# Expert rows written to DRAM in slot order ahead of the experts, loaded back in quarters of the partitions and transposed by VectorE

## The reference

```python
def _moe_forward(x, gate_w, w_gate_up, w_down, shared_w_gate_up, shared_w_down):
    x2 = x.reshape(-1, orig_shape[-1])
    g_s, u_s = jnp.split(x2 @ shared_w_gate_up.T, 2, axis=-1)
    shared_out = jax.nn.silu(g_s) * u_s @ shared_w_down.T
    probs = jax.nn.softmax(x2 @ gate_w.T, axis=-1)
    topk_vals, topk_idx = jax.lax.top_k(probs, 2)
    topk_vals = topk_vals / jnp.sum(topk_vals, axis=-1, keepdims=True)
    combine = jnp.sum(jax.nn.one_hot(topk_idx, 16) * topk_vals[..., None], axis=1)
    g, u = jnp.split(jnp.einsum('th,eih->eti', x2, w_gate_up), 2, axis=-1)
    out_e = jnp.einsum('eti,ehi->eth', jax.nn.silu(g) * u, w_down)
    return (jnp.einsum('eth,te->th', out_e, combine) + shared_out).reshape(orig_shape)

x = x + tanh(g_xattn[0]) * xattn(layernorm(x), ctx, ...)
x = x + tanh(g_ffn[0]) * ffn(layernorm(x), ...)
```

## Time and profile before

| | |
|---|---|
| time, median of 3 runs | 1397.36 us (1397.26 to 1397.74) |
| profiled execution | 1397.51 us, of which 1395.8 us are its span |
| busy share of the span | PE 99%, DVE 72%, ACT 37%, POOL 26% |
| expert blocks | from 1198 to 1345 us of the span |
| granted TensorE clock, mean | 0.999 |

### The profile page before, as it was taken

How to read it: one execution, slowest core, us unless ns; L and a number is a source line. 1 busy time by engine, 2 the same in 40 slices (tenths; PEclk the granted TensorE clock), 3 DMA queues, 4 the chain that set the end, 5 groups by cost and what they waited for, 6 DMA issues and landing times.

```text
span 1395.8 us, 26753 instructions
## 1 busy us (share of the span) xinstructions
PE 1382.0 (99%) x8757; PEld 1121.7 (80%) x8758; DVE 1000.4 (72%) x2135; ACT 514.6 (37%) x1117; POOL 358.0 (26%) x374
## 2 busy tenths in 40 slices
PE   9999999999999999999999999999999999999998
PEld 7888887888888887888887888888787888777777
DVE  6444456888888888888888888888688746244458
ACT  5333444333333434343333333343434331222242
POOL 1121223221212121212211121212122100367646
PEclk9999999999999999999999999999999999999999
DMA  6544431111111111111101111111123244555548
GB/s 220 189 128 143 128 109 44 39 42 31 49 31 43 39 42 32 43 40 41 43 30 47 36 42 32 49 31 42 54 72 98 99 151 174 188 196 165 165 154 298
DMA packets 91238, 125.52 MB, mean 90 GB/s; under 512 B 7184, under 2 KB 57360, under 8 KB 90896
## 3 DMA queue, kind: packets, MB, share of 16 engines
q1 hardware_dynamic: 83632, 99.70, 22.7%
q0 software_dynamic: 7520, 24.65, 5.3%
HBM read 86.84 MB, written 37.49 MB: 89 GB/s over the span
## 4 chain that ended last, share of the span: by engine, by line
PE 79%; DVE 3%; issue 1%; DMA 1%; ACT 0%; DVEq 0%; POOL 0%; SPq 0%; ACTq 0%
PE ps L609 19%; PE ps L611 18%; PE ps L610 18%; PE ps L1004 6%; PE ps L696 5%; PE ps L743 4%; PE ps L1020 3%; PE ps L728 2%; PE ps L999 1%; DVE acc L1960 1%; DVE acc L1967 1%; DMA y<-ybuf 1%; PE ps L917 1%; PE ps L751 0%; PE ps L1051 0%
## 5 line engine op out<-in xcount | busy, mean ns | idle before, releaser
L506 POOL CAST vth<-vt 128x256 fp32r<-128x256 f32 x64 | 25.4, 397 | 541.4 <-PE ps L743 539.4
L1194 ACT CAST ah<-ps 128x256 fp32r<-128x256 f32 x256 | 83.4, 383 | 187.5 <-PE ps L611 181.0
L609 PE MATMUL ps<-hT,w0h 128*128 128x512 f32 (+1 forms) x384 | 152.2, 396 | 0.0
L611 PE MATMUL ps<-hT,w0h 128*128 128x512 f32 (+1 forms) x384 | 149.9, 390 | 0.0
L610 PE MATMUL ps<-hT,w0l 128*128 128x512 f32 (+1 forms) x384 | 149.6, 390 | 0.0
L500 POOL TENSOR_TENSOR qr<-qv,mhalf 128x8 f32<-128x8 f32 x64 | 105.1, 1642 | 151.5 <-DVE qv L1560 124.3
L1511 DVE TENSOR_TENSOR acc<-ps,acc 128x512 f32 (+1 forms) x128 | 88.0, 687 | 56.6 <-PE ps L611 56.4
L1160 ACT COPY qs<-ps 128x512 f32<-128x512 f32 x128 | 75.3, 588 | 122.6 <-PE ps L611 122.6
L1172 ACT ACTIVATE pb<-pb 128x256 f32<-128x256 f32 x128 | 48.3, 418 | 167.0 <-DVE pb L1578 166.9
L609 PE MATMUL ps<-w0l,ah 128*128 128x512 f32 x256 | 105.6, 413 | 0.0
L609 PE MATMUL ps<-w1l,ah 128*128 128x512 f32 x256 | 104.9, 410 | 0.0
(11 more groups left out here) (250 smaller groups left out, 3216.1 us busy)
## 6 DMA issues: line engine op xcount, KB each, us to landing
wraw<-in_w_att SPq DMA_DIRECT2D x64, 256.0 KB, 2.7
vbuf<-vo SPq DMA_DIRECT2D x16, 512.0 KB, 3.3
kbuf<-ko SPq DMA_DIRECT2D x16, 512.0 KB, 3.8
kt<-kbuf SPq DMA_DIRECT2D x32, 256.0 KB, 2.9
vt<-vbuf SPq DMA_DIRECT2D x64, 128.0 KB, 2.2
wgu<-in_w_gu SPq DMA_DIRECT2D x4, 2048.0 KB, 9.0
y<-ybuf SPq DMA_DIRECT2D x16, 512.0 KB, 7.1
xt<-in_x SPq DMA_DIRECT2D x16, 256.0 KB, 4.2
```

Source lines behind the costliest of these rows:

```text
L609: pe.matmul(dst, l_hi, r_lo, start=first, stop=False)
L611: return pe.matmul(dst, l_hi, r_hi, start=False, stop=last)
L1194: act.copy(ah[:, bp, :, b2, :], pv_view(bp, b2)).then_inc(a_hi, 1)
```

## The change

Instead of gathering each block's rows by an index just ahead of their use, the kernel writes all rows to DRAM in slot order once. After the slot numbers are known, GpSimd scatters each token tile twice (for the first and the second expert) from four row buffers `rows` in SBUF to `xbuf`, 32 indirect DMAs by `sli`. SP loads those tiles from `h2buf` into `rows`: the first four when the logits have been transposed, the others as scatters of the buffer's last tile have landed (`rows_out`). `rows` lies in memory that place 0 of `act_raw` uses later, so VectorE waits for all scatters ahead of `shared_in(3, 0)`. Slots which no token fills must hold finite numbers, so SP copies rows of `x` over the whole of `xbuf` during attention, 28 copies of 512 KB.

A block is then loaded by SP with plain DMAs, one for each quarter q of 32 partitions. To make that enough, `h2` tiles are stored with their columns in another order (`by_quarter`): the four values of the four parts of the width stand side by side. A quarter of a row in DRAM is then what 32 partitions of the transposed block need, and VectorE turns each block with one 32x32-block transpose (`turn_rows`), straight into `xgT`. TensorE's four transposes and ScalarE's copy go, and ScalarE copies the down product to `ye` in VectorE's place.

Around it: the logits' transposes stand half a step earlier on TensorE, and `shared_in(1, 1)` stands behind the first part of the routing on VectorE. The last shared step runs its first part for both halves first, after which `xgT` may be written. Some semaphores are joined to keep their number; these waits ask for the same events as before.

```diff
+    xbuf = nc.dram_tensor("xbuf", [(STEPS - NC) * P, D], F32, kind="Internal").ap()
+    x_rows = xbuf.rearrange("(b g i) (q n) -> b q i g n", g=4, i=32, q=4)
+    x_pair = xbuf.rearrange("(d r p) n -> d r p n", r=2, p=P)
...
+        with ExitStack() as a:
+            sb("below_rows", [P, 2 * 4096], F32, a)
+            rows = [sb(f"rows{q}", [P, D], F32, a) for q in range(4)]
...
+        def by_quarter(t):
+            return t.rearrange("p (m k) -> p k m", k=KD)
+        def in_order(t):
+            return t.rearrange("p (k m) -> p k m", k=KD)
...
             with sp.Fori(0, (STEPS - NC) // 2) as d:
                 for odd in range(2):
                     next_loads(d, odd)
+                sp.dma_start(x_pair[d], x[0:2]).then_inc(x_in, 16)
...
+            def load_rows(n):
+                if n >= 4:
+                    sp.wait_ge(rows_out[n % 4], 32 * (n // 4))
+                sp.dma_start(rows[n % 4][:], h2_t[n]).then_inc(rows_in[n % 4], 16)
+
+            def load_block(b, j):
+                if not isinstance(b, int) or b >= 3:
+                    sp.wait_ge(xgT_done, b - 2)
+                for q in range(4):
+                    src = x_rows[b, q] if isinstance(b, int) else x_rows[bass.ds(b, 1), q].rearrange(
+                        "a i g n -> (a i) g n")
+                    sp.dma_start(xg[j % 3][32 * q:32 * q + 32, :].rearrange("p (g n) -> p g n", g=4), src).then_inc(
+                        xg_in[j % 3], 16)
...
-            pool.wait_ge(sidx_ok, 1)
-            for q in range(4):
-                pool.wait_ge(h2_stored[q], 16 * (NT // 4) + 16)
-            def gather(b):
...
+            pool.wait_ge(slot_ok, 1)
+            for n in range(NT):
+                pool.wait_ge(rows_in[n % 4], 32 + 16 * (n // 4))
+                for z in range(2):
+                    pool.indirect_dma_start(xbuf, bass.IndirectOffsetOnAxis(sli[:, z, n:n + 1], 0),
+                                            rows[n % 4][:], None).then_inc(rows_out[n % 4], 16)
...
-                    mm = pe.transpose(PS[bank][:, k * P:(k + 1) * P], h2_tile(n)[:, k * P:(k + 1) * P], ident[:])
+                    mm = pe.transpose(PS[bank][:, k * P:(k + 1) * P], by_quarter(h2_tile(n))[:, k], ident[:])
...
-            def expert_T(b, rounds, j):
-                pe.wait_ge(xg_in[j % 3], 16 * rounds + 16 * (j // 3) + 16)
...
-                pe.wait_ge(xgT_evac, b + 2)
+                pe.wait_ge(xgT_done, b + 2)
...
-                act.activation(h2_tile(n), acc[:, n, :], ACT.Identity, bias=nb3[:, n:n + 1],
+                act.activation(by_quarter(h2_tile(n)), in_order(acc[:, n, :]), ACT.Identity, bias=nb3[:, n:n + 1],
...
+            def act_block(b, q, first=False):
+                if not isinstance(b, int) or b + 1 < NB:
+                    act.wait_ge(e_act, b + 1)
+                    silu(b + 1, 1 - q)
+                act.wait_ge(ed_done, b + 1)
+                if not first:
+                    act.wait_ge(y_st[q], 8 * (b - q))
+                act.copy(ye[q][:], PS[5 + q][:]).then_inc(ye_ok, 1)
...
-            for it in range(4):
+            for q in range(4):
+                dve.wait_ge(rows_out[q], 32 * 4)
+            for it in range(3):
                 shared_in(3, it)
+
+            def turn_rows(b, q, rounds, j):
+                dve.wait_ge(xg_in[j % 3], 64 * rounds + 64 * (j // 3) + 64)
+                if not isinstance(b, int) or b >= 2:
+                    dve.wait_ge(eg_done, b - 1)
+                dve.transpose(xgT[q][:].rearrange("p k (g i) -> p g k i", g=4),
+                              xg[j % 3][:].rearrange("p (g j k) -> p g k j", g=4, k=KD)).then_inc(xgT_done, 1)
...
-            def dve_block(b, q, first=False):
+            def dve_block(b, six, j):
+                q = j % 2
+                gated(b, q)
+                if not isinstance(b, int) or b + 2 < NB:
+                    turn_rows(b + 2, q, 2 * six, j + 2)
                 dve.wait_ge(eT_done, b + 1)
                 dve.tensor_copy(acteT[:], PS[4][:, 0:P]).then_inc(eT_evac, 1)
```

169 lines of the change are left out of this document (84 added, 85 removed).

## The result

The changed kernel takes **1425.59 us** (median of 4 runs, 1425.14 to 1430.86), against 1397.55 (1397.26 to 1398.69) of the kernel before on the same chip: a ratio of **1.0208 [1.0183, 1.0232]**. It is 28 us slower, where I had forecast 5; the time lies outside the range. The profiled execution has a span of 1423.9 us, 28.1 more than before.

What follows compares the result with a forecast made beforehand. TensorE, busy throughout the expert loop and alone on its chain, was taken to bound the kernel. The terms - 20.5 + 20.4 + 2.0 + 2.2 + 0.7 = + 4.8 us gave a forecast of 1402 us, range 1392 to 1410.

Steps and rivals of the forecast that it cites:

- transposes off TensorE: All 188 transposes leave TensorE at 0.109 us each, 20.5 us in all; a block falls from 3.14 to 2.70 us.
- stall at step (3,2): Ahead of the experts, TensorE waits until the last scatter lands at about 1206: 20.4 us (15.4 to 23.4).
- slow restart: After the long stop TensorE comes back slowly: 2.0 us, between 0 and 5.4.
- first blocks: Block 3's rows queue behind the last 2 MB of gate-up weights and come late: 2.2 us (0 to 3.1), once.
- a loop paced by another engine: Rival: SP's four issues over 2.70 us or VectorE's turn over 1.6 pace the expert loop; 1416 us, chance 0.09.
- my signs: Step (3,0) some 25 us late behind a DMA, TensorE idle 15 to 23, scatter gaps from the 25th, blocks at 2.70.
- GpSimd's pace: Floor for the 32 scatters ahead of the experts: one each 0.99 + 0.30 us, the last landing at 1201.
- SP's order: Late rows wait in SP's queue among weights; row 15 at up to 1205, the last scatter down between 1201 and 1209.
- my floor: The stall ahead of step (3,2) if GpSimd's scatter pace alone decides: 15.4 us.
- Cost 0: Filler copies in SP's queue, and operations on every fourth float (normalisation, `h2` transposes, turn), were each put at no cost.
- every fourth float is slow: Rival: TensorE's load of strided `h2` tiles takes twice as long over 64 transposes, + 7, 1409 us; chance 0.13.
- rows keep up: Rival: row 15 lands by 1197, the stall is 15.4; 1395 us, or 1393 without the late block 3; chance 0.20.

Runs made afterwards that it cites:

- e8: Against e7: VectorE builds the one-hot matrices behind the scatters of tile 14, TensorE's counts stand half a step earlier; 1421.88 us, ratio 1.0173.
- e5: Changed kernel with row tiles 4 to 15 loaded in a row and 4 MB of weights behind the loads of blocks 0 to 2; 1421.64 us, ratio 1.0171.
- e6: Changed kernel with each 512 KB filler copy asked for between the two attention steps of SP's loop; 1422.52 us, ratio 1.0179.
- e4: Changed kernel with the columns of `h2` stored in their own order (wrong values, same work); 1423.92 us, ratio 1.0186.
- e3: Changed kernel with blocks 3 and 4 asked for ahead of the gate-up weights of experts 12 to 15; 1422.84 us, ratio 1.0175.
- e2: Changed kernel with `rows` in the memory of later down weights, so step (3,0) waits for no scatter; 1420.01 us, ratio 1.0157.
- e10: e9 without the 180 small products on TensorE; 1413.28 us, ratio 1.0107.
- e7: Changed kernel with `rows` apart, row tiles in a row, filler moved, 7 MB of weights issued by ScalarE after the scatters, TensorE waiting for them; 1425.44 us, ratio 1.0201.
- e9: Against e8: VectorE waits for late weights, one-hot matrices follow tile 13, late weights reordered, TensorE runs 180 small products while waiting; 1415.41 us, ratio 1.0132.

## Why the prediction was wrong

Right in direction and place, wrong in size by 23 us. Its terms:

| term | forecast | measured |
|---|---|---|
| transposes off TensorE | -20.5 | -19.6 in the blocks, -0.9 ahead of them |
| lag ahead of the stretch (copies, stride) | 0 | +5.6 |
| stall at step (3,2) | +20.4 (15.4 to 23.4) | +30.9 |
| slow restart | +2.0 | +2.2 |
| first blocks | +2.2 (0 to 3.1) | +6.1 |
| rest of the loop | 0 | +4.0 |
| end | +0.7 | -0.3 |
| sum | +4.8 | +28.0 (span +28.1) |

- **What is removed** held. A block takes 2.70 us; 180 of the 188 transposes stood behind the experts' start, 19.6 us at 0.109. VectorE's turn (1.10 us, I had 0.71), SP's four loads and GpSimd's scatters are hidden in the loop, so the rival of a loop paced by another engine falls. Of my signs the trace of after shows the long gap ahead of step (3,2), a DMA behind it, gaps among the late scatters and blocks at 2.7; but the product of step (3,0) begins 40.9 us later and not 25, the gap is outside the 15 to 23 that I gave, and the first late row is that of tile 10.
- **The stall** is the largest miss, 10.5 us. By the steps of the forecast: the first scatter started 0.92 us behind `sli` where I had 0.51, 0.4 more. The 16th scatter, on which row 11 waits, was to start 19.35 us behind the first and started 24.8 behind it (1163.92 to 1188.70). The pace was a little better than my 1.29, but the four scatters beside the one-hot operations cost 5.6; e8 takes those operations away, and the slowness goes. That is the step that failed: "GpSimd's pace" came from the earlier trace rows, a scatter that happened to have no such operation beside it, and I gave nothing for what VectorE does there. The 16th scatter's landing took 1.1 more. Then "SP's order": I bounded the queue from row 11 to row 15 by 13 and 24 us (the 13 was itself short: 5.25 MB at 369 GB/s are 14.2), and took 21.6 (1206 - 4.2 - 1180.2). It took 25.2, from 1192.7 to 1217.9, a little over the upper end: the bytes were nearly right, 9.1 MB against 8.9, and so was the rate, 365 GB/s against the 369 of the earlier trace rows. At a share of 0.97 there was nothing idle in that stretch that would have justified less. So 0.4 + 5.4 + 1.1 + 3.6. That the whole of the 5.4 would come back with quick scatters is argued, since no run changed them alone. e5 bears both sizes out: its stall is my floor and the 5.6 of the slow scatters, and the weights add 9.5 to it in after, where I had added 5.0.
- **The slow restart** came out nearly as sized: ten products, each 0.2 us longer, the first a little more.
- **"Cost 0" was wrong in two places.** The filler copies cost about 3 us through TensorE's gap at the loop's turn (e6). I looked at SP's queue and the rate for them, not at what else asks for DMA. The stride costs 1.7 us (e4) through ScalarE's normalisation and the load of weights from strided `h2`. My rows were two small VectorE operations; the strided load of weights goes from 141 to 210 ns, so half of the rival "every fourth float is slow" was there. The rival priced it on TensorE alone, at 7 us. The Trainium skill, page "SBUF — State Buffer", section "Door 1: The DMA port swizzle", states a penalty for each new 16-byte line. The traces agree: the normalisation goes from 0.80 to 1.28 us on ScalarE and from 0.54 to 0.74 on VectorE, and both go back in e4. For the turn, 1.10 against 0.709, the stride as the cause isn't shown.
- **Block 3** was foreseen and mis-sized. Its rows landed 7.32 us after their issue and were turned 10.6 us after the experts' start; I had written 8.5 to 10.2, though my terms (7 to 9, 1 and 0.7) add up to 8.7 to 10.7. That cost 3.03 idle (e3 gives 2.75 back). But four products that follow the idle stretch take 2.07 us instead of 1.13, and blocks 0 to 4 together lost 6.1.
- **A cover that went.** In after five blocks, each the first of a round of the loop, take 0.35 to 0.48 us longer than 2.70. Before, the longer ones stand 0.04 to 0.13 above 3.14; the difference makes some 1.6 us. That the loop's branch costs this on TensorE's queue, and that the transposes hid it before, is my reading; no run tests it. Blocks 10 and 11 lose another 0.5. Ahead of block 44's down product TensorE waits 1.26 us for an activation which VectorE makes late, behind a split of the shared activation (L1997); with the slow products behind it that is 1.9. I costed the removal as pure gain, and did not ask what the transposes covered.
- **The rival "rows keep up"** falls for after. e5 brings the rows in time and shows a stall of 21.26, not 15.4, because of the slow scatters. Without these the time would still not have been 1395: the weights that were put off came due at the experts.

The deeper fault is one of framing. I treated the wait at step (3,0) as the price of the change, and asked when the last row comes. e2 takes the wait away and gets 5.6 us. As far as the runs show, the price is the traffic itself: rows read once and written twice ahead of the experts, in a stretch that also loads the weights.

## What to carry to other kernels

When a change moves work from an engine into transfers ahead of a stage, add up all bytes that must be down before the stage can run, weights too, and divide by a rate that the trace shows under load; an order of the queue can't beat that, it only says who waits. A wait that you find on the path may be a symptom: ask what would be late next if it were gone, and price that before you price the wait. And what you take off the busiest engine may have been covering small things there, such as a branch or a late copy: look for them at every place where it stood.

## What was not expected of the hardware

- An indirect DMA on GpSimd whose index lies in SBUF takes 0.96 us, and 1.82 to 2.58 beside VectorE operations on two SBUF operands, of 1504 or 2048 elements a partition, that run at its start (after, and 2.39 in e10 at another place); it ends 0.8 to 1.1 us behind them.
- Copies from DRAM to DRAM of 512 KB, 28 of them, went with a gap of 2.84 us on TensorE where a long loop comes round and where before has none; issued a step away from it, they leave no gap (e6). That late instruction packets are the cause is inferred.
- Where TensorE reads from memory which count to wait for, it stood idle for 0.3 to 0.8 us a block, and a block took 3.3 to 3.7 us instead of 2.70 (e7, e8). With the same reads on VectorE, which has spare time, those gaps are gone (e9); ahead of block 0 they still cost the path some 0.9 us (e10).
- Products that TensorE runs only to stay awake brought nothing where a wait of 9 us still followed them: it came back at a granted clock of 0.60 (e9).
